# Two small router steps moved to the end of their DVE step, the keys' transfers split into two signals, and the last additions shared between two engines

## The reference

```
x = x + window_attention(group_norm(x))      # 16 heads of 32, windows of 8 x 8, masks, relative positions
t = t + attention(layer_norm(t))             # 8 heads of 16 over the 256 tokens of an image
t = t + mixture_of_experts(layer_norm(t))    # 8 experts, hidden 256, the 2 best by router score
```

```
logits = x @ router_w.T + router_b
topk_val, topk_idx = top_k(logits, 2)
weights = softmax(topk_val)                  # 1 / (1 + exp(second - first)) and the rest
onehot = one_hot(topk_idx, 8)
out = sum over the 2 chosen experts of weight * (silu(h1) * h2 @ fc2.T + fc2_b)
```

## Time and profile before

| | us |
|---|---|
| median of 3 runs | 778.26 |
| lowest and highest | 772.68, 778.88 |
| the profiled execution's own time | 770.44 |
| its span in the trace | 768.6 |

### The profile page before, as it was taken

The page is one execution under the profiler, slowest core; times in us unless marked ns, Lnnn a source line. Parts: engine busy times, 40 slices in busy tenths (PEclk is TensorE's granted clock), DMA queues, the critical chain, the costliest instruction groups (busy, mean ns, idle before and its releaser), DMA issues. The chain is left out here.

```text
span 768.6 us, 20244 instructions
## 1 busy us (share of the span) xinstructions
PE 643.4 (84%) x7046; PEld 543.4 (71%) x7046; DVE 518.1 (67%) x1513; ACT 503.8 (66%) x1427; POOL 485.9 (63%) x556
## 2 busy tenths in 40 slices
PE   3887989999989899898998989888776699999910
PEld 2766878777778777787777878776564688888800
DVE  4666767888788878878878788884453456566524
ACT  3555788878778777888778887765551166666600
POOL 6354656665767786687867867675465436666645
PEclk9799999999999999999999999999997799999965
DMA  7102013031331303313032230312462213333246
GB/s 198 34 3 35 6 32 70 30 99 20 88 77 41 102 24 93 68 54 102 23 92 48 77 101 23 92 41 77 125 213 92 67 51 93 87 85 93 74 160 195
DMA packets 48074, 59.27 MB, mean 77 GB/s; under 512 B 10370, under 2 KB 41218, under 8 KB 47458
## 3 DMA queue, kind: packets, MB, share of 16 engines
q1 hardware_dynamic: 41846, 45.65, 22.5%
q0 software_dynamic: 4544, 9.38, 3.6%
q10 hardware_dynamic: 1584, 2.95, 1.0%
HBM read 36.00 MB, written 28.64 MB: 84 GB/s over the span
## 5 line engine op out<-in xcount | busy, mean ns | idle before, releaser
L587 POOL TENSOR_TENSOR pb<-pb,rcb 128x512 f32<-128x512 f32 x128 | 156.5, 1223 | 149.8 <-DVE rcb L873 148.5
L628 POOL DMA_INDIRECT ysl<-yo,dst x78 | 75.5, 968 | 58.4 <-DVE yo L1147 42.4
L739 ACT ACTIVATE pb<-pSB,mxb 128x256 f32<-128x256 f32 x128 | 59.5, 469 | 47.2 <-DVE mxb L973 46.6
L739 ACT ACTIVATE pb<-pSA,mxb 128x256 f32<-128x256 f32 x128 | 59.6, 475 | 41.2 <-DVE mxb L973 41.2
L1266 PE MATMUL pTB<-ident,pb 128*128 128x128 f32 x512 | 80.2, 280 | 7.2 <-ACT ptb L753 7.1
L595 POOL TENSOR_TENSOR pa<-pa,rca 128x512 f32<-128x512 f32 x64 | 67.2, 1050 | 28.5 <-DVE rca L1038 28.5
L753 ACT ACTIVATE ptb<-pTB 128x512 f32<-128x512 f32 x128 | 77.1, 602 | 2.0 <-PE pTB L1266 2.0
L523 POOL DMA_INDIRECT slots<-rec,slot x64 | 65.3, 1020 | 15.5 <-issue 14.1
L1266 PEld LDWEIGHTS pTB<-ident,pb 128*128 128x128 f32 x512 | 57.9, 142 | 11.1 <-issue 7.8
L759 ACT ACTIVATE pta<-pTA 128x512 f32<-128x512 f32 x64 | 38.6, 603 | 40.3 <-PE pTA L1358 40.1
L973 DVE TENSOR_REDUCE mxb<-pSB 128x2 f32<-128x512 f32 x64 | 43.9, 686 | 21.1 <-PE pSB L1235 21.0
(11 more groups left out here) (221 smaller groups left out, 1996.5 us busy)
## 6 DMA issues: line engine op xcount, KB each, us to landing
slots<-sel_dram SPq DMA_DIRECT2D x16, 1040.0 KB
kbd<-kst SPq DMA_DIRECT2D x128, 64.0 KB, 2.4
xt<-slots SPq DMA_DIRECT2D x39, 130.0 KB, 2.2
xch<-x_ch_dram SPq DMA_DIRECT2D x4, 512.0 KB, 7.1
xt<-x_tok_dram SPq DMA_DIRECT2D x16, 128.0 KB, 2.4
xch<-t SPq DMA_DIRECT2D x16, 128.0 KB, 2.1
fw<-f_dram SPq DMA_DIRECT2D x1, 2048.0 KB
yc<-ysl SPq DMA_DIRECT2D x8, 256.0 KB, 7.4
```

Of the source, the lines that this page charges most:

```text
L587: pool.tensor_tensor(pb[:, b, :, :], pb[:, b, :, :], rcb[:, b, :].unsqueeze(2).to_broadcast([128, 2, TOK]), ALU.mult).then_inc(sb_nrm, 1)
L628: pool.indirect_dma_start(ysl, bass.IndirectOffsetOnAxis(ap=dst[:, t % YB, n:n + 1], axis=0), yo[:, t % YB, n, :], None).then_inc(y_dma[t ...
L739: last = a.activation(pb[:, b, qc, :], (pSB, pSA)[n % 2][:, qc * TOK:(qc + 1) * TOK], ACT.Exp, bias=mxb[:, b, qc:qc + 1], accum_out=smb[:, ...
```

## The change

It does three things, and renames some semaphores of the group norm (waits for DVE's own results, now counted on one semaphore; the waits are the same and stand at the same places).

1. `chose` and `rden` keep their step, but stand at its end on DVE, behind the work of the other phases.
2. SP issues the eight key transfers in the order 0, 4, 1, 5, 2, 6, 3, 7. The first four count on `k1_dma`, the last four on the new `k1_far`. PE waits for the first at step 0 and for the second at step 2. ACT, before it writes the next keys, waits for both.
3. POOL adds the second result for the even groups only; DVE does it for the odd ones. SP waits for each group on the semaphore of its engine.

```diff
-                    for h in range(8):
+                    for h in (0, 4, 1, 5, 2, 6, 3, 7):
                         rows = slice(D1 * h, D1 * h + D1)
                         sp.dma_start(kbd1[M.par][rows, :, :, h % 4, :].bitcast(f32), kst1[rows, :, :, :].bitcast(f32))\
-                          .then_inc(k1_dma[M.par], 16)
+                          .then_inc((k1_dma, k1_far)[h % 4 // 2][M.par], 16)
...
-                sp.wait_ge(o_two, g + 1)
+                sp.wait_ge((o_even, o_odd)[g % 2], g // 2 + 1)
...
-            for g in range(NGRP):
+            for g in range(0, NGRP, 2):
                 pool.wait_ge(o_one, g + 1)
-                pool.tensor_tensor(yc[:, 0, g, :], yc[:, 0, g, :], yc[:, 1, g, :], ALU.add).then_inc(o_two, 1)
+                pool.tensor_tensor(yc[:, 0, g, :], yc[:, 0, g, :], yc[:, 1, g, :], ALU.add).then_inc(o_even, 1)
...
-                        wait(a, k1_dma[(M.par + 1) % 2],
-                             (M.half + M.par) * 128 if M.j > 0 else 0)
+                        for moved in (k1_dma, k1_far):
+                            wait(a, moved[(M.par + 1) % 2], (M.half + M.par) * 64 if M.j > 0 else 0)
...
-                last.then_inc(gn_st, 1)
-                v.wait_ge(gn_st, part)
+                last.then_inc(gn_own, 1)
+                v.wait_ge(gn_own, 5 * part - 4)
...
-                    if L is not None and n == 5:
-                        v.wait_ge(q_top, L.j * 3 + 2)
-                        if K is not None:
-                            v.wait_ge(q_mine, K.j + 1)
-                        v.tensor_tensor(chose[:, :, :, :], iota[:, :].unsqueeze(1).unsqueeze(1).to_broadcast([128, 2, 2, E]),
-                                        ix8[:, :, 0:2].rearrange("p s k -> p k s").unsqueeze(3).to_broadcast([128, 2, 2, E]),
-                                        ALU.is_equal).then_inc(q_top, 1)
-                    if L is not None and n == 7:
-                        v.wait_ge(q_exp, L.j + 1)
-                        v.tensor_scalar(rden[:, :, :], rexp[:, :, :], 1.0, None, ALU.add).then_inc(q_den, 1)
...
                     if R is not None and n == 5:
                         v.wait_ge(r_ag, R.j + 1)
                         v.tensor_scalar(rs2[:, :], mv2[:, :, 1], EPS, None, ALU.add).then_inc(r_eps, 1)
+                    if L is not None and n == 5:
+                        v.wait_ge(q_top, L.j * 3 + 2)
+                        if K is not None:
+                            v.wait_ge(q_mine, K.j + 1)
+                        v.tensor_tensor(chose[:, :, :, :], iota[:, :].unsqueeze(1).unsqueeze(1).to_broadcast([128, 2, 2, E]),
+                                        ix8[:, :, 0:2].rearrange("p s k -> p k s").unsqueeze(3).to_broadcast([128, 2, 2, E]),
+                                        ALU.is_equal).then_inc(q_top, 1)
+                    if L is not None and n == 7:
+                        v.wait_ge(q_exp, L.j + 1)
+                        v.tensor_scalar(rden[:, :, :], rexp[:, :, :], 1.0, None, ALU.add).then_inc(q_den, 1)
...
                 v.tensor_tensor(yc[:, 0, g, :], yc[:, 0, g, :], res2[:, g * GRP:(g + 1) * GRP], ALU.add).then_inc(o_one, 1)
+                if g % 2 == 1:
+                    v.wait_ge(o_one, g + 1)
+                    v.tensor_tensor(yc[:, 0, g, :], yc[:, 0, g, :], yc[:, 1, g, :], ALU.add).then_inc(o_odd, 1)
...
-                            pe.wait_ge(k1_dma[Bm.par], Bm.half * 128 + 128)
+                            pe.wait_ge(k1_dma[Bm.par], Bm.half * 64 + 64)
+                        if n == 2:
+                            pe.wait_ge(k1_far[Bm.par], Bm.half * 64 + 64)
```

More of the change, by code:

```diff
@@ L297, in hybrid_kernel @@
             sem(n) for n in ("c_w0h", "c_w0l", "c_wvh", "c_wvl", "c_w1s", "c_w1h", "c_w1l", "c_bq", "c_bias"))
-        gn_st, gn_ag, gn_sq, gn_e2, gn_mm, gn_cp, gn_q, gn_v, gn_eps, gn_pow = (
-            sem(n) for n in ("gn_st", "gn_ag", "gn_sq", "gn_e2", "gn_mm", "gn_cp", "gn_q", "gn_v", "gn_eps", "gn_pow"))
+        gn_own, gn_e2, gn_mm, gn_cp, gn_eps, gn_pow = (
+            sem(n) for n in ("gn_own", "gn_e2", "gn_mm", "gn_cp", "gn_eps", "gn_pow"))
         x_c, x_s, x_h, x_l = sem("x_c"), sem("x_s"), sem("x_h"), sem("x_l")
@@ L308, in hybrid_kernel @@
         k1_dma = [sem("k1_dma0"), sem("k1_dma1")]
+        k1_far = [sem("k1_far0"), sem("k1_far1")]
         m_xb, m_o, m_t, m_st, m_ag, m_eps, m_pow, m_tn, m_T, m_hi, m_lo, m_k, m_khi, m_klo, m_q, m_qhi, m_qlo = (
@@ L328, in hybrid_kernel @@
         o_dma = sem("o_dma")
-        e_w, e_x, e_xT, e_h1, e_h2, e_sil, e_gat, e_y, y_ev, y_T, y_w, e_dst, o_one, o_two = (
+        e_w, e_x, e_xT, e_h1, e_h2, e_sil, e_gat, e_y, y_ev, y_T, y_w, e_dst, o_one, o_even, o_odd = (
             sem(n) for n in ("e_w", "e_x", "e_xT", "e_h1", "e_h2", "e_sil", "e_gat", "e_y", "y_ev", "y_T", "y_w",
-                             "e_dst", "o_one", "o_two"))
+                             "e_dst", "o_one", "o_even", "o_odd"))
         zeros_d = sel_d.rearrange("p k -> (p k)")[64 * E * 128:64 * E * 128 + TOK * ROW]
@@ L825, in statistics @@
                     last = v.bn_stats(gst[:, j, :], xch[:, j * TOK:(j + 1) * TOK])
-                last.then_inc(gn_st, 1)
-                v.wait_ge(gn_st, part)
+                last.then_inc(gn_own, 1)
+                v.wait_ge(gn_own, 5 * part - 4)
                 for j in images:
                     last = v.bn_aggr(gmv[:, j, :], gst[:, j, :])
-                last.then_inc(gn_ag, 1)
-                v.wait_ge(gn_ag, part)
+                last.then_inc(gn_own, 1)
+                v.wait_ge(gn_own, 5 * part - 3)
                 t = slice(images.start, images.stop)
-                v.tensor_tensor(gsq[:, t], gmv[:, t, 0], gmv[:, t, 0], ALU.mult).then_inc(gn_sq, 1)
-                v.wait_ge(gn_sq, part)
+                v.tensor_tensor(gsq[:, t], gmv[:, t, 0], gmv[:, t, 0], ALU.mult).then_inc(gn_own, 1)
+                v.wait_ge(gn_own, 5 * part - 2)
                 v.tensor_tensor(gmv[:, t, 1], gmv[:, t, 1], gsq[:, t], ALU.add).then_inc(gn_e2, 1)
@@ L843, in group_variance @@
                 v.wait_ge(gn_cp, part)
[L844 to L847, removed]
+                v.tensor_tensor(gsq[:, t], gsum[:, t, 0], gsum[:, t, 0], ALU.mult).then_inc(gn_own, 1)
+                v.wait_ge(gn_own, 5 * part - 1)
+                v.tensor_tensor(gsq[:, t], gsum[:, t, 1], gsq[:, t], ALU.subtract).then_inc(gn_own, 1)
+                v.wait_ge(gn_own, 5 * part)
                 v.tensor_scalar(gsq[:, t], gsq[:, t], EPS, None, ALU.add).then_inc(gn_eps, 1)
```

## The result

| | before | changed |
|---|---|---|
| median of 4 runs each, us | 776.3 | 754.0 |
| lowest to highest, us | 772.68 to 778.88 | 750.1 to 757.44 |
| the profiled execution, us | 770.44 | 750.1 |
| its span, us | 768.6 | 748.3 |

What follows compares the result with a forecast made beforehand. No engine sets the pace alone; a loop through several does. Gains of 9.0 (`rden`), 1.4 and 1.2 (`chose`), 5.5 (keys) and 1.9 (last additions) sum to 19.0 us: from 778.26 to 759 us, range 751 to 769.

Steps and rivals of the forecast that it cites:

- the forecast itself: Whole kernel: all gains sum to 19.0 us, giving 759 us; chance 0.6 for 755 to 763.
- What waits for POOL: DVE instructions reading SBUF only, or with two SBUF inputs, and POOL tensor instructions don't overlap; the second waits for the first.
- `rden`: forecast 0.75 an image, 9.0: DVE ahead of `q`: moved, it takes 0.15 us and `q` starts earlier, 0.63 to 0.93 us in 12 images.
- The second `ahead`: DVE behind the moved `rden`: pushed some 0.08 us, it often just misses and waits for POOL's `pb` to end at 392.22.
- `chose`: forecast 0.12 an image, 1.4: DVE step 5: the move frees 0.95 us, but POOL's gapless work lets only 0.13 through, in 12 images.
- The rival of another chain: POOL's run of steps 4 to 6 holds the loop; gain only 12 us in all, 766 us; chance 0.15.
- `chose` at 566 us: DVE beyond the full pipeline: 1.96 us through two `pb`; moved, it can meet one, gain 1.2 us (0.7 to 1.8).
- Keys: Ahead of PE's scores: two transfer groups remove 5.5 of 6.1 us of waiting beyond 0.69; bounds 3 and 6.1.
- Final additions: Kernel's end: sharing POOL's last additions with DVE takes 6.3 us against 8.2, gain 1.9 (1.4 to 2.4).
- Semaphores of the group norm: Group norm: the renamed semaphores have the same waits, so 0 us.
- Doubly blocked: End of step 5: `chose` waits for two POOL instructions, 7.4 us less gain, still faster, 766.7 us; chance 0.12.
- slower: Moved instructions wait through a whole POOL run: 1.6 us per image lost, 11.8 us slower in all, 790; chance 0.05.

Runs made afterwards that it cites:

- the second weight: Changed kernel with the product of `rec` and `rexp` on DVE moved from step 2 to the end of step 1: 754.08 us, ratio 0.9720.
- its three variants: Changed kernel with the second weight moved (754.08 us); with POOL's `t1b` moved to step 7 and step 5's `rcb` on DVE (756.57); with both edits (757.09).

## Why the prediction was right, and where it wasn't

The time, 754.0, lies in the range, 1 us below the 755 to 763 given for the forecast itself. Most steps hold, but that the sum came so close is partly luck: two terms were too large by 2.9 us together, three were too small by 1.5, and the clock, which the forecast didn't have, helped the changed kernel in the profiled pair. Term by term:

**What waits for POOL.** The prediction said that any DVE instruction that reads SBUF only waits. That is too wide. In the trace of before, reductions `mxa` of 128x512 start while POOL's `pb` or `pa` runs and take 0.67 us, and the reciprocal of `rden` (L911) takes 0.16 there in 11 images. The reduction in place of `rden` tested it.

**`rden`: forecast 0.75 an image, 9.0; measured 0.60, 7.2.** The mechanism was right: 0.15 in its new place, the gain on the path to PE. The size is near the lower bound, 0.63, which I had from ACT's high part of the queries, and `q` is indeed held by it in the changed kernel, 0.26. I had lifted the term to 0.75 because an earlier `chose` would bring `kst` 0.6 us forward and ACT with it; counted from the start of `pa`, `kst` comes 0.09 earlier (4.85 instead of 4.94). The second `ahead` was hit as foreseen, but in 3 of 12 images (1.04), and takes 0.17 in the others.

**`chose`: forecast 0.12 an image, 1.4; measured 0.05 in eleven images with the keys alone (0.10, 31.73 to 31.63, with `rden` too) and 0.91 (0.75) in the first, 1.5 to 1.8.** Right number, wrong reason. I said that 0.95 us are freed and POOL's run lets only 0.13 through. In fact 0.10 is freed: the slot cast behind it waits instead, 1.01. The first image, which has no cast, is the counter-test: there the whole 0.95 is freed and nearly all of it comes through. The order of before and after, with `CAST slot` right behind `chose`, had this in it: I asked what the moved instruction would meet in its new place, and not which one of the same kind would now stand in the old one. The rival of another chain named POOL's run as holding all. It falls, since 0.60 an image came through for `rden` with that run unchanged.

**`chose` at 566 us: forecast 1.2; measured 0.1.** The same mistake: the cast takes 1.94 in its place. The drain of the pipeline, to the last `slots` scatter, is 112.48 us with the keys alone and 111.11 with keys and `chose`, but 1.2 us of that difference lie behind `t`, where the granted clock was 0.81 in one execution and 0.91 in the other.

**Keys: forecast 5.5; measured 6.3 (4.4 to 8.2).** In the trace of before the waits beyond 0.69 are 3.3 in 14 images, 0.5 in the next and 3.24 - 0.93 = 2.3 in the last, 6.1, the sum of which the prediction took 5.5. Not forecast: what the key wait would have eaten of `rden`, 4.5 us. I added the two as if they were independent. The sum came out right only since both were made; `rden` alone is worth less than its term. Nor did I have the clock's fall, 2.4 us of the 5.8 in the first three iterations.

**Final additions: forecast 1.9; measured 2.0 and 2.2 in the traces, 2.8 (1.4 to 4.2) by the ratio.** From the last four residuals on, the changed kernel takes 5.8 us (735.35 to 741.16), where 8.2 stood before and 6.3 were forecast. The turns are as worked out: 12 x 0.62 + 4 x 1.04 = 11.6 for all additions, measured 11.57. The warning of the Trainium skill (Perfetto Trace Analysis, Optimizing Scalar/DVE Operations) that moving work between the two might not help didn't come true here: the engines do take turns, but DVE's turn is the shorter one.

**Semaphores of the group norm: forecast 0.** Not tried by itself.

**Not in the forecast: the experts' stage, 5.0 us longer** in the changed kernel's trace.

With 7.2, 1.8, 0.1, 6.3 and 2.2 the terms measured come to 17.6, where 19.0 were forecast; the medians say 22.3, with an interval of 17 to 27. What the clock's falls add can't be put on top, since the 6.3 come from medians and hold them as far as those runs had them.

The one pair of traces can be accounted for, with the trace of the keys alone between them. Of the 25.3 us outside the experts' stage 0.9 lie ahead of the first image's fillers, 10.4 come with the keys (2.4 of these the clock's fall at the first image), 9.1 with the two moves, and 2.6 at the end. The last 2.3 lie behind the late `chose`, where the granted clock was 0.81 over 18 us before and 1.00 after. They can't be counted as the change's: one of its variants (the second weight) shows that stretch as long as before, 37.3 us against 37.0.

*Doubly blocked* falls: `chose` takes 0.19 in all images, also where it had met the two `pb` of the earlier trace rows. So does *slower*, since nothing that was moved waited through a run of POOL.

**Open: the experts' tiles.** A tile takes 3.03 us. In the nine traces of before and of the kernels built from it, all tiles but the first two do, and the stage takes 133.9 to 135.4. In all five traces of the changed kernel and its three variants 5 to 9 later tiles take 3.2 to 6.3, and the stage 138.9 to 143.0. Timelines of DVE, ACT and PE in the changed kernel:

```profile
625.63 0.41 DVE L1148 TENSOR_TENSOR yo<-pM,xt 128x256 f32<-128x256 f32 x1
630.48 0.42 DVE L1122 COPY xs<-pG 128x256 f32<-128x256 f32 x1 [4.44 <-remote]
...
630.54 0.47 ACT L802 ACTIVATE yt<-pOA,ws 128x256 f32<-128x256 f32 x1 [3.33 <-remote]
...
627.84 0.38 PE L1461 MATMUL pM<-ident,yt 128*128 128x128 f32 x2
631.01 1.61 PE L1440 MATMUL pSB<-xs,ws 128*128 128x256 f32 x4 [2.79 <-issue]
```

Three engines stand still together, and no event in the trace releases them. Two readings are open. Either the changed kernel does it: it alone has all parts and the merged semaphores of the group norm. Or it belongs to the occasion: the five traces come from the two sessions in which the kernel before also took 776, and eight of the nine from those in which it took 767 to 768, a difference of the size of these stops. The ninth, the trace of before without stops, speaks for the first reading; but it was that kernel's fastest execution there, 770.44 beside 772.68 to 778.88, so the others may have had them. The ratios speak for the second reading. Keys and `rden` had 0.9789, and `chose` and the final additions should take some 4 us more off, to about 0.974. Stops of 5 to 9 us that only the changed kernel has would have given 0.980 to 0.985; it had 0.9715 and 0.9737, with intervals that end at 0.9781 and 0.9792. That is an argument and not a test. A trace of before from the third session would have told them apart, and so would the changed kernel with the old semaphores; neither was taken.

## What to carry to other kernels

Where two engines take turns, moving the instruction that waits moves the wait to the next one of its kind in the old place: read the row behind it before pricing the move, or write it in a form that doesn't wait (here a reduction in place of an addition, the same gain without any move). Two waits ahead of the same consumer aren't additive: shortening the path to PE was worth 1.9 us while the keys came late, 4.5 us of it being lost in their wait, and 7.2 in the traces once they came in time, so remove the later one first. And a wait in the trace is not yet the loop: the 0.56 us that DVE waited less for POOL came back whole as a wait for ACT. Before a difference between two traces is put down to an edit, compare the granted clock of the stretch in which it lies.

## What the runs showed of the hardware

- A cast of 128x4 and an addition on 128x2 in SBUF wait on DVE until POOL's running `pb` ends, 1.01 and 1.00 us instead of 0.16 and 0.15; a reduction of 128x4 in the same place takes 0.15 while `pb` runs.
- The clock's fall to 0.50 behind one and the same PE wait (scores 1.99 us behind the fillers) came in some executions and not in others (0.50 in 76 to 80 us in one, 1.00 in another), and cost 2.4 us. In none of nine traces with scores 0.69 behind the fillers did it come.
- In the drain of the pipeline the granted clock over the same 18 us of work was 0.81, 0.91 or 1.00 from one execution to another, and the time from there to the last scatter into the slots 34.8 to 37.3 us.
- Stops of up to 4.4 us of DVE, ACT and PE together, released by nothing in the trace, add up to 5 to 9 us in the experts' stage of five traces and are in none of nine.
